# One product for q and k of a half in the causal attention stage, and what ScalarE reads of it

## The reference, cut to what matters

```python
x = x + _L1_attn_ref(_layernorm(x, axis=-1), L1_attn_wq, L1_attn_bq, L1_attn_wk, L1_attn_bk, ...)

def _L1_attn_ref(x, wq, bq, wk, bk, wv, bv, wo, bo):
    q = x @ wq + bq            # wq, wk, wv: 128 x 64
    k = x @ wk + bk
    v = x @ wv + bv
    w = jnp.einsum('bqh,bkh->bqk', q, k) * (1.0 / math.sqrt(64))
    w = w + mask               # causal
    w = jax.nn.softmax(w, axis=-1)
    z = jnp.einsum('bqk,bkh->bqh', w, v)
    return z @ wo + bo
```

## Time and profile before

| | us |
|---|---|
| median of 3 runs | 1986.97 |
| lowest and highest of the 3 | 1983.47, 1987.98 |
| the profiled execution's own time | 1987.98 |
| its span, first to last instruction | 1986.2 |
| busy in the span: PE, DVE, ACT, POOL | 1589.5, 1734.1, 1599.0, 1500.9 |
| causal stage, from the first transposition of batch 0 to that of batches 1, 2, 3 | 47.97, 95.70, 143.45 |
| end of the causal stage (last addition to x) | 1899.1 |

### The profile page before, as it was taken

One profiled execution on the slowest core, in us unless ns is written; L12 is line 12 of the kernel. 1 busy time (PEld: TensorE's weight loads), 2 busy tenths in 40 slices (PEclk: granted clock), 3 DMA queues, 4 the chain that ended last, 5 costly groups with the idle time before them and its releaser, 6 DMA issues. The chain is left out here.

```text
span 1986.2 us, 26727 instructions
## 1 busy us (share of the span) xinstructions
PE 1589.5 (80%) x8579; PEld 555.5 (28%) x8579; DVE 1734.1 (87%) x3742; ACT 1599.0 (81%) x1374; POOL 1500.9 (76%) x1026
## 2 busy tenths in 40 slices
PE   3788888877888888788888888888888877899966
PEld 1122222222222222222222222222222244466655
DVE  5889999998999999989999999999999488755556
ACT  2799999999999999989999999999999511222243
POOL 3999999998999999989999999999999111000010
PEclk7799999999899999999999999999999888877778
DMA  3110000000100000010000000000000000000001
GB/s 87 42 44 13 16 16 13 13 13 28 30 13 14 15 16 13 13 39 19 13 13 13 15 17 13 13 13 15 17 13 7 1 1 0 0 0 1 1 0 43
DMA packets 32491, 33.12 MB, mean 17 GB/s; under 512 B 5657, under 2 KB 23136, under 8 KB 32352
## 3 DMA queue, kind: packets, MB, share of 16 engines
q1 hardware_dynamic: 30117, 30.12, 5.0%
q10 hardware_dynamic: 2235, 1.28, 0.3%
HBM read 22.74 MB, written 8.39 MB: 16 GB/s over the span
## 5 line engine op out<-in xcount | busy, mean ns | idle before, releaser
L1028 POOL TENSOR_TENSOR sigma_weights<-grown 128x1024 f32<-128x1024 f32 x480 | 912.1, 1904 | 0.0
L680 DVE TENSOR_SCALAR sigma_weights<-ps_sig 128x512 int32<-128x512 int32 x1024 | 691.4, 675 | 62.5 <-PE ps_sig L473 61.8
L926 ACT ACTIVATE tau_weights<-ps_tau 128x1024 f32<-128x1024 f32 x506 | 694.0, 1372 | 30.2 <-PE ps_tau L485 30.1
L912 ACT ACTIVATE sigma_weights<-sigma_weights,kernel_shape 128x2048 f32<-128x2048 f32 x256 | 601.8, 2351 | 27.9 <-POOL sigma_weights L1028 27.9
L689 DVE TENSOR_TENSOR running_max<-ps_sig,running_max 128x512 f32<-128x512 f32 x896 | 605.1, 675 | 0.0
L1001 POOL TENSOR_SCALAR grown<-sigma_weights,kernel_shape 128x1024 f32<-128x1024 f32 x480 | 542.7, 1131 | 62.2 <-DVE sigma_weights L680 61.3
L921 ACT ACTIVATE sigma_weights<-sigma_weights 128x2048 f32<-128x2048 f32 x256 | 578.9, 2261 | 0.1
L527 PE MATMUL ps_acc<-tau_weights,v_heads 128*9 128x512 f32 x2048 | 536.4, 603 | 6.0 <-DVE sums L706 5.0
L527 PE MATMUL ps_acc<-sigma_weights,v_heads 128*9 128x512 f32 x2048 | 539.3, 606 | 0.0
L485 PE MATMUL ps_tau<-q_operand,k_operand 128*128 128x512 bf16 x1012 | 308.6, 387 | 185.2 <-ACT tau_weights L926 178.3
L473 PE MATMUL ps_sig<-q_operand,k_operand 96*128 96x512 bf16 x1024 | 403.1, 394 | 58.9 <-DVE running_max L689 36.3
(11 more groups left out here) (193 smaller groups left out, 1439.7 us busy)
## 6 DMA issues: line engine op xcount, KB each, us to landing
q_operand<-q_parts SPq DMA_DIRECT2D x192, 48.0 KB
k_operand<-k_parts SPq DMA_DIRECT2D x63, 144.0 KB
q_parts<-parts SPq DMA_DIRECT2D x24, 128.0 KB, 2.4
k_parts<-parts SPq DMA_DIRECT2D x18, 128.0 KB, 2.4
x_res<-in_L_attn_x SPq DMA_DIRECT2D x8, 256.0 KB, 4.1
q_operand<-max_rows SPq DMA_DIRECT2D x128, 2.0 KB
out<-x_res SPq DMA_DIRECT2D x4, 512.0 KB, 3.2
k_parts<-parts ACTq DMA_DIRECT2D x6, 128.0 KB, 2.8
```

Of the source, the lines that this page charges most:

```text
L680: dve.tensor_scalar(sig[:, g % SIG_RING, cols].bitcast(I32), ps_sig[:, half, :].bitcast(I32), SIGN_OFF, None, ALU.bitwise_and).then_inc(ma ...
L912: act.activation(chunk(c), chunk(c), ACT.Ln, bias=shape[:, CHUNK * c // TB % H, 1:2]).then_inc(ln_done, 1)
L926: act.activation(tau[:, g % TAU_RING, :], (ps_tau, ps_sig)[tau_bank(g)[0]][:, :, :].rearrange("p h q -> p (h q)"), ACT.Exp, scale=float(DH ...
L1028: pool.tensor_tensor(sig[:, g % SIG_RING, :], t, t, ALU.mult).then_inc(sq_ready, 1)
```

## The change

q and k of a half come from one product. The still matrix is wq and wk side by side, 128 columns, so the 512 tokens are streamed once; q comes out in partitions 0 to 63 and k in partitions 64 to 127 of one bank, `ps_s[:, 1, g, :]`. `proj_ready` rises once for each half, and `take_qk` waits once. ACT reads q and k as before in two instructions of 64x512; that of k reads partitions 64 to 127 and writes partitions 0 to 63 of `qk_c`. Its bias must lie beside its input, so the column bk is loaded to partitions 64 to 127.

```diff
-        w["b1"] = sb("b1_cols", [DA, 2])
+        w["b1"] = sb("b1_cols", [P, 2])
...
-                    (w["b1"][:, 0:1], column("L1_attn_bq")), (w["b1"][:, 1:2], column("L1_attn_bk")),
+                    (w["b1"][0:DA, 0:1], column("L1_attn_bq")), (w["b1"][DA:P, 1:2], column("L1_attn_bk")),
...
             def take_qk(b, g):
 
+                act.wait_ge(proj_ready, b * 2 + (g + 1))
                 for s in range(2):
-                    act.wait_ge(proj_ready, b * 4 + (2 * g + s + 1))
-                    act.activation(qk[:, s, g * HALF:(g + 1) * HALF], ps_s[0:DA, s, g, :], ACT.Identity,
-                                   bias=w["b1"][:, s:s + 1]).then_inc(qk_ready, 1)
+                    rows = slice(s * DA, (s + 1) * DA)
+                    act.activation(qk[:, s, g * HALF:(g + 1) * HALF], ps_s[rows, 1, g, :], ACT.Identity,
+                                   bias=w["b1"][rows, s:s + 1]).then_inc(qk_ready, 1)
...
                     pe.wait_ge(zt_ready, b * 2 + (g + 1))
-                    for s in range(2):
-                        pe.matmul(ps_s[0:DA, s, g, :], w["qkv1"][:, s, :], zt[:, g * HALF:(g + 1) * HALF],
-                                  start=True, stop=True).then_inc(proj_ready, 1)
+                    pe.matmul(ps_s[:, 1, g, :], w["qkv1"][:, 0:2, :].rearrange("p s d -> p (s d)"), zt[:, g * HALF:(g + 1) * HALF],
+                              start=True, stop=True).then_inc(proj_ready, 1)
```

## The result

The changed kernel takes 2026.14 us in the median (2010.08 to 2027.19, 4 runs) against 1987.47 (1983.47 to 1989.43, 4 runs). The ratio is 1.0173, with a 95% interval of 1.0147 to 1.0199: 34 us slower by the ratio, 39 between the medians, as one of the four runs took 2010. The forecast was 9 us faster, and its range, 1974 to 1985, does not hold the time. The profiled execution took 2025.87 us with a span of 2024.1.

What follows compares the result with a forecast made beforehand. PE alone was taken to bound the causal stage. 5.7 us from the first half plus 3.1 from the second gave 8.9 us off the profiled 1987.98: 1979.1 there, 1978.1 against the median of 1986.97; range 1974 to 1985.

Steps and rivals of the forecast that it cites:

- What bounds the stage: Causal stage, start of a batch: PE runs without a gap, DVE and ACT wait for it, so PE alone sets the time.
- the first half: Tokens 0 to 511: one of two products goes and v ends earlier, saving 5.7 us over four batches, bounds 4.0 and 8.6.
- case (a): First half: clock still rises 5.3 us after the first transposition, v ends at 6.40, saving 1.00 us; taken for batch 0.
- The cover on ACT: First half: both ACT copies end at 5.14 us, under v, done at 5.26 to 6.40, so they cost nothing.
- The second half: Between scores(0) and scores(1) a 0.93 us product goes; ACT's idle before the second exponential limits the saving to 3.1 us in all.
- The costs taken as nothing: 128 still columns, ACT's copy of k across partitions (0.68 us as now) and bk's load elsewhere: nothing added.
- The sum: Causal stage, four batches: 5.7 us from the first half plus 3.1 from the second, 8.9 us saved.
- the middle of two bounds: First half, batches 1 to 3: clock rise 5.3 or 2.84 us after the first transposition, saving 1.00 or 2.14; 1.57 taken.
- the clock does not rise in time: First half: with less wide streaming v runs wholly slow; 1.5 us lost a batch, kernel at 1993; chance 0.07.
- The rival of a missing rise in one or two batches only: Start of one or two batches: late clock rise, each costing 3 to 4 us, kernel at 1981 to 1985; chance 0.18.
- a row from another stage: Tree stage: leaf transpositions alone, with no product, brought the clock up in 2.84 us; set against the late-rise rival.

Runs made afterwards that it cites:

- run 12: Changed kernel plus unread products: first half of batch 0; three ahead of scores(7), three short at the end, batches 0 to 2: 1970.45 us.
- run 9: Kernel before plus unread products in batches 0 to 2: three ahead of scores(7), three short ones at the batch's end: 1993.53 us, ratio 1.0024.
- run 1: Changed kernel with its 128-column product issued a second time, unread, in both halves of each batch: 1988.08 us, ratio 1.0001.
- Runs 2: Changed kernel with a second, unread 128-column product in the first half only (tokens 0 to 511): 2019.64 us, ratio 1.0158.
- run 3: Changed kernel with a second, unread 128-column product in the second half only (tokens 512 to 1023): 1998.78 us, ratio 1.0061.
- run 7: Kernel before plus three unread products (128 columns, 512 tokens) in the 3.07 us wait ahead of scores(7), batches 0 to 2: 1971.75 us, ratio 0.9910.
- run 11: Kernel before plus three unread products ahead of scores(7), as in run 7, but over 32 rows instead of 128: 1986.87 us, ratio 0.9994.
- run 8: Changed kernel plus unread products: first half of batch 0; ahead of tile 1's transpositions; three ahead of scores(7), three short at the end, batches 0 to 2: 1956.46 us.
- run 5: Kernel before without q's product: one 64-column product for each half, both copies read k's result, output differs: 2026.75 us, ratio 1.0187.

## Why the prediction was wrong, point by point

*What bounds the stage* was right: PE alone sets the time. So was *the first half*, as far as batch 0 goes. With the rise 5.37 us after the first transposition, v ended at 6.49; case (a) said 6.40. *The cover on ACT* held: both copies were done at 1723.69, v at 1724.68. *The second half* was right in size: the idle time of 0.83 ahead of the second exponential is gone, which came 9.73 us after the first transposition instead of 11.55. *The costs taken as nothing* added nothing that can be seen: the copy's median was 683 ns against 678. The product between scores(0) and scores(1) took 1.06 us from its start to the next (1725.02 to 1726.08), 0.13 more than the 0.93 counted, but there ScalarE is what the second exponential waits for.

*The sum was right where the clock is held.* Batches at 2.4 GHz throughout take 37.14 and 37.26 us with the single product (run 12) and 38.73 with the two (run 9): 1.5 to 1.6 us. For such batches the working gives 0.93 for a product at full clock and 0.77 for the second half, 1.7.

*The step that failed* is the clock, twice. First, for batches 1 to 3 I took the middle of two bounds on when it rises. In batches 2 and 3 that was sound: the rises at 3.55 and 3.61 us lie between the bounds, and v ended at 5.54 and 5.58. In batch 1 the clock did not rise at the start at all. Neither bound came from a start with half of its wide products.

Second, and for more of the time, nothing in the prediction asked whether the clock would stay up. The working counted 0.93 us at full clock as taken away between scores(0) and scores(1), and did not see that the streaming taken away had helped to keep the clock up through the wait and the narrow scores behind it. Before, the clock held there in all four batches, and so it did in the four of run 1 (mean clocks 0.75 and 0.90, as before). In the changed kernel it fell there in all three batches in which it had risen. Runs 2 and 12 put the fall of batch 0 at the same place, in the scores of tile 3. That product is not the whole of it: in batch 0 of run 3 and batch 2 of run 9 it stood in its place and the clock fell there too.

*The rival* "the clock does not rise in time" was this mechanism in its first half, and its sign was right. Its price was not: I gave 1.5 us a batch, as though the clock came up a little later. The price is that of a batch mostly at 1.2 GHz, 6.6 to 14.1 us measured, 36.3 in all instead of 6. This could have been read off before: PE was busy for 42.8 to 43.0 us of 47.7 in a batch of which half already ran at 1.2 GHz, so there was little idle time to hide a slower other half. Batch 3 had the largest loss, as it was at full clock the longest before. The rival of a missing rise in one or two batches only came true for the rise itself, in batch 1; its price of 3 to 4 us was too low in the same way, and it did not foresee the falls. The rival of a clock that does not rise in time, at a chance of 0.07, was also far too unlikely; what I set against it was a row from another stage.

*The Trainium skill's* rule ("TensorE: Matmul & The Clock Gate", Part 4) that transpositions do not engage the full clock was set beside the earlier trace rows, which still speak against it. The rule pointed to the right danger; the rows refuted the rule and not the danger. The section "HAM oscillation" of the same page of the Trainium skill lays the fall of the clock to idle gaps between bursts of matmuls. The trace agrees in that the clock fell in the wait of 3.07 us and held when run 7 filled it. It is not the idleness alone, though: run 11 filled the same wait with products over 32 rows and the clock fell, and in batch 0 of the changed kernel the clock fell with no wait over 0.67 us, and PE was busy for 52.55 of 54.58.

What stays open: whether the clock falls in a given batch depends on more than the batch's own code. Batches with the same instructions took 46 and 54 us in one execution (runs 2 and 3), batches 1 and 2 of run 9 38.73 and 51.43, and the changed kernel itself ran in 2010 once and in 2026 three times. I have not tried to steer where a batch starts against the changes of the clock.

## What to carry to other kernels

Where TensorE is the bound and its clock moves between its two levels, first price the stage at either level over its whole length; then ask of every product that is removed, or made to run beside another, whether the clock needed it. A version with unread products in place of the removed ones costs one run and tells the two effects apart. Put such products into waits that exist anyway, and measure each set: all of them together gave 33 us here (run 8), but the three short ones at the end of a batch, added to the kernel before without the one ahead of the transpositions of tile 1 (run 9 against run 7), lost 22.

## What the runs showed of the hardware that I had not expected

- Two products of 64 columns with outputs on different halves of the partitions run side by side: four instructions in 1.98 us against 3.57 with both outputs on partitions 0 to 63, both at 1.2 GHz.
- Work that takes TensorE the same time doesn't do the same for the clock. Three products over 32 rows took 2.84 us and did not hold it; three over 128 rows took 2.84 us and did (runs 11 and 7: 1986.87 against 1971.75). The number of still columns made no such difference: the changed kernel with 128 took 2026.14, run 5 with 64 and as many instructions 2026.75.
- Once down, the clock can stay down for long though PE does not idle. In batch 2 of run 9 it was at 1.2 GHz from 1808.94 to 1836.24, 27 us in which the profile shows PE busy throughout, and then it rose in the middle of the batch. Why then is not shown.

```profile
1809.00:1836.00 27.00, 27.00 (x78) 0.50 0.00 0
1836.00:1837.00 1.00, 1.00 (x3) 0.88 0.06 16
```
